# Routing of twelve of sixteen tiles moved into the attention ahead of it, in a two-layer attention and mixture-of-experts kernel

## What is computed

```
x = x + attention0(layernorm(x), ctx)      # similarity attention over 1024 context rows
x = x + experts0(layernorm(x))             # 12 gate logits a row: 8 experts, 4 "zero" experts
x = x + attention1(layernorm(x), ctx, mask)# 4 heads of 64
x = x + experts1(xf = that x)              # 8 gate logits; gelu MLP behind a layer norm per expert

logits = x_n @ gate (+ bias)               # experts0; experts1 likewise
top2, idx = top_k(logits, 2);  g = softmax(top2)
out = sum over the two picked experts of g * (act(x_n @ w1[e]) @ w2[e])
```

## Time and profile before

| | us |
|---|---|
| median of 3 runs | 1073.15 |
| lowest, highest | 1072.77, 1074.06 |
| the profiled execution | 1080.48 |
| its span, first to last instruction | 1078.5 |
| TensorE busy | 911.1 |
| VectorE busy | 624.1 |
| ScalarE busy | 511.2 |
| GpSimd busy | 421.2 |

### The profile page before, as it was taken

One profiled execution on the slowest core, in us unless ns is written; L12 is line 12 of the kernel. 1 busy time (PEld: TensorE's weight loads), 2 busy tenths in 40 slices (PEclk: granted clock), 3 DMA queues, 4 the chain that ended last, 5 costly groups with the idle time before them and its releaser, 6 DMA issues. The chain is left out here.

```text
span 1078.5 us, 19681 instructions
## 1 busy us (share of the span) xinstructions
PE 911.1 (84%) x6248; PEld 804.9 (75%) x6249; DVE 624.1 (58%) x1368; ACT 511.2 (47%) x1097; POOL 421.2 (39%) x352
## 2 busy tenths in 40 slices
PE   0579989977699997058999989897778999999996
PEld 0468979866499996047778778786648999999995
DVE  2456354326655556847878878786755444444443
ACT  1243233115344443047768767664744555555552
POOL 0445243100255553063625536321032555555542
PEclk9989999986799999579999999999689999999998
DMA  5352110007466663530001100000965666666662
GB/s 176 93 181 79 37 42 2 1 1 249 132 215 228 231 232 105 162 131 11 30 21 43 37 20 21 1 26 21 319 233 179 197 198 195 195 199 200 207 193 34
DMA packets 67570, 131.46 MB, mean 122 GB/s; under 512 B 7824, under 2 KB 50192, under 8 KB 62384
## 3 DMA queue, kind: packets, MB, share of 16 engines
q1 hardware_dynamic: 55024, 110.13, 30.0%
q0 software_dynamic: 12480, 20.48, 8.1%
HBM read 108.95 MB, written 21.64 MB: 121 GB/s over the span
## 5 line engine op out<-in xcount | busy, mean ns | idle before, releaser
L1604 PEld LDWEIGHTS d_hps<-d_xg_t,d_xw 128*128 128x128 f32 x1248 | 149.2, 196 | 7.1 <-DVE d_xg_t L1786 5.7
L1604 PE MATMUL d_hps<-d_xg_t,d_xw 128*128 128x128 f32 x1248 | 149.8, 280 | 5.0 <-DVE d_xg_t L1786 5.0
L1513 ACT ACTIVATE x<-d_hps,b 128x128 f32<-128x128 f32 x312 | 89.0, 368 | 123.9 <-PE d_hps L1604 118.9
L683 POOL TENSOR_SCALAR c_prob<-c_prob,c_rinv 128x1024 f32<-128x1024 f32 x64 | 71.4, 1123 | 140.8 <-DVE c_rinv L1083 140.4
L1614 PE MATMUL d_yps<-d_w,d_hid_hi 128*128 x312 | 116.8, 406 | 2.3 <-DVE d_hid_lo L1795 2.3
L1439 POOL DMA_INDIRECT out_x<-d_y,d_take_slot x39 | 67.3, 1725 | 111.1 <-DVE d_y L1823 60.7
L1090 DVE TENSOR_TENSOR c_pt_lo<-c_tp,c_pt_hi 128x512 fp32r<-128x512 f32 x128 | 82.1, 683 | 5.0 <-ACT c_pt_hi L939 4.7
L1617 PE MATMUL d_yps<-d_w,d_hid_lo 128*128 x312 | 82.0, 283 | 0.0
L1076 DVE CUSTOM_DVE_ANT_0 c_prob<-c_sc,c_minf 128x1024 f32<-128x1024 f32 x64 | 75.6, 1219 | 8.4 <-PE c_sc L750 6.3
L1604 PEld LDWEIGHTS b_hps<-b_xg_t,b_w 128*128 128x128 f32 x624 | 76.6, 195 | 4.6 <-issue 2.4
L1604 PE MATMUL b_hps<-b_xg_t,b_w 128*128 128x128 f32 x624 | 78.4, 280 | 1.3 <-DVE b_xg_t L1783 0.7
(11 more groups left out here) (344 smaller groups left out, 2223.7 us busy)
## 6 DMA issues: line engine op xcount, KB each, us to landing
d_xw<-in_w SPq DMA_DIRECT2D x39, 1024.0 KB
b_w<-in_w SPq DMA_DIRECT2D x47, 512.0 KB, 7.5
d_w<-in_w SPq DMA_DIRECT2D x8, 1024.0 KB, 11.6
a_raw<-in_ctx_t SPq DMA_DIRECT2D x4, 1024.0 KB, 5.4
a_raw<-in_ctx SPq DMA_DIRECT2D x4, 1024.0 KB, 5.5
ybuf<-a_zero SPq DMA_DIRECT2D x2, 2048.0 KB, 14.2
b_ysum<-ybuf SPq DMA_DIRECT2D x8, 512.0 KB, 8.3
c_ctx_t<-in_ctx_t SPq DMA_DIRECT2D x14, 256.0 KB, 3.1
```

The lines of the kernel that those rows point to most:

```text
L683: nc.gpsimd.tensor_scalar(prob[w][:], prob[w][:], rinv[:, w:w + 1], 1.0, ALU.mult, ALU.mult).then_inc(s["prob_ready"], 1)
L1513: op = nc.scalar.activation(hid[q][:, h * FH + c, :], src[:, c, :], ACT.Gelu_apprx_tanh, bias=b1[:, ds(e, 1), h * FH + c])
L1604: mm = nc.tensor.matmul(hps[j % 2][h][:, c * P:(c + 1) * P], w1[j % WL][:, k, at:at + P], xg_t[j % 2][:, k, :], start=(k == 0), stop=(k == ...
```

## The change

The sixteen tiles are split: the first TE = 12 "early" ones and four "late" ones.

1. In each attention's last steps, where the `x` of batches 0 to 2 is final, the early tiles get statistics, normalised rows (six each on VectorE and ScalarE in `attention0`; eight on ScalarE and four on VectorE in `attention1`), transposes (`turn_rows`), logits (`early_logits`) and, on VectorE, the top two (`top_two`). The rows go to DRAM from there. Square root and exponential sit in different tables of ScalarE, which are loaded for each. What routing needs (`gw`, `pick`, `top`, `idx`, `load`) now lives outside the blocks.
2. The experts blocks begin with the early tiles' ranks, while the late tiles are normalised; GpSimd makes the 24 early one-hot lanes, VectorE the eight late ones. The chain over all sixteen tiles follows as before, with `expert_of` behind the lanes.
3. `w2`'s low parts are made in order of experts: 0 to 2 on TensorE and ScalarE, 3 to 5 on VectorE, 6 and 7 on GpSimd inside the first two steps of the loop. `down` of the first six blocks waits only for its own expert's part. SyncE loads `w2` 0 and 1, the late rows, 2 to 5, then `w1` of the first blocks, then 6 and 7.
4. The scaling of `x` for the zero experts is done in steps 0 to 5 of the first loop, from `x` and its statistics (`own`, `off`).
5. To make room in `attention1` the mask is loaded tile by tile into two buffers.

```diff
+                def turn_rows(i):
+                    bank = (sc[:, 0:512], sc[:, 512:1024], tp[0][:])[i % 3]
...
+                def early_logits():
+                    pe.wait_ge(s["gate_in"], 32)
+                    for i in range(2):
+                        turn_rows(i)
+                    for i in range(TE // 2):
+                        if i + 2 < TE // 2:
+                            turn_rows(i + 2)
+                        pe.wait_ge(s["row_t"], i + 1)
+                        for a in range(2):
+                            t = 2 * i + a
+                            for k in range(KD):
+                                at = (a * KD + k) * P
+                                mm = nc.tensor.matmul(tp[1][:, t * 12:(t + 1) * 12], xn_t[i][:, at:at + P], r.gw[:, k, :],
+                                                      start=(k == 0), stop=(k == KD - 1))
+                    mm.then_inc(s["logit_done"], 1)
 
                 def step(b, q, t, before, now, nxt):
...
+                    if not now and t == 2:
+                        early_logits()
...
+                    if not now and t == 0:
+                        act.wait_ge(s["stat"], 6)
+                        nc.scalar.activation(m.std[:, slice(0, TE)], m.var[:, slice(0, TE)], ACT.Sqrt, bias=m.const[:, C_EPS:C_EPS + 1]
+                                             ).then_inc(s["sqrt_done"], 1)
+                        nc.scalar.activation(m.spare1[:], m.const[:, C_EPS:C_EPS + 1], ACT.Exp)
+                        act.wait_ge(s["stat"], 8)
+                        act.wait_ge(s["raw_lo"], 4 * B)
+                        for n in range(DVE_ROWS, TE):
+                            nc.scalar.activation(row_tile(n), m.x[:, n, :], ACT.Identity, scale=m.rstd[:, n:n + 1],
+                                                 bias=m.nmr[:, n:n + 1]).then_inc(s["row_act"], 1)
+                    if not now and t == LAST:
+                        for i in range(TE // 2):
+                            act.wait_ge(s["row_tp"], i + 1)
+                            nc.scalar.activation(xn_t[i], (sc[:, 0:512], sc[:, 512:1024], tp[0][:])[i % 3], ACT.Copy).then_inc(s["row_t"], 1)
                     if now and t == 0:
                         split_high(2 * b + 1, cn_hi[q])
...
+                def early_route():
+                    after(nc.vector.tensor_tensor(logit[:], tp[1][:, 0:TE * 12].rearrange("p (t e) -> p e t", e=12),
+                                                  r.ebias[:].unsqueeze(2).broadcast_to([P, 12, TE]), ALU.add))
+                    after(top_two(nc, m, r, after, 12, slice(0, TE), logit[:], logit2[:], grid[:]))
 
                 def step(b, q, t, before, now, nxt):
                     p, g = b - 1, b * TB + t
@@ -465,6 +574,14 @@
                             dve.wait_ge(s["pt_hi"], g * 2 + half - 1)
                             nc.vector.tensor_tensor(pt_lo[:, js, tile * P:(tile + 1) * P], tp[half][:].rearrange("p (j i) -> p j i", i=P),
                                                     pt_hi[:, js, tile * P:(tile + 1) * P], ALU.subtract).then_inc(s["pt_lo"], 1)
+                    if not now and t == 0:
+                        dve.wait_ge(s["bn_done"], B - 1)
+                        stats_chain(nc, m, dve, s["stat"], s["sqrt_done"], slice(0, TE))
+                        nc.vector.scalar_tensor_tensor(m.nmr[:, slice(0, TE)], m.mean[:, slice(0, TE)], -1.0, m.rstd[:, slice(0, TE)],
+                                                       ALU.mult, ALU.mult).then_inc(s["stat"], 1)
+                        dve.wait_ge(s["raw_lo"], 4 * B)
+                        for n in range(DVE_ROWS):
+                            normalise(nc, m, row_tile(n), n).then_inc(s["row_dve"], 1)
                     if now:
...
+                def early_logits(q):
+                    pe.wait_ge(s["row_t_act"], q + 1)
+                    pe.wait_ge(s["row_t_dve"], q + 1)
+                    for t in range(TB):
+                        n = q * TB + t
+                        for k in range(KD):
+                            mm = nc.tensor.matmul(sc[0][:, n * E:(n + 1) * E], row_t[q][:, k, t * P:(t + 1) * P], r.gw[:, k, :],
+                                                  start=(k == 0), stop=(k == KD - 1))
+                    mm.then_inc(s["logit_done"], 1)
+
                 pe.wait_ge(s["xn_ready"], TB)
                 for k in range(KD):
                     turn_x(k, tp[k])
@@ -880,17 +1035,35 @@
                     if more:
                         pe.wait_ge(s["k_lo"], b * 4 + 6)
                         q_proj(0, xb)
+                    else:
+                        pe.wait_ge(s["x_ready"], b * 2)
+                        turn_rows(0, 0, xb[:])
                     turn(b, 6, 0)
                     values(b, 4)
+                    if not more:
+                        pe.wait_ge(s["row_t_act"], 1)
+                        turn_rows(0, 1, xb[:])
                     turn(b, 6, 1)
 
                 turn(B - 1, 7, 0)
+                pe.wait_ge(s["row_t_dve"], 1)
+                pe.wait_ge(s["max_done"], B * UP * 2)
+                turn_rows(1, 0, xb[:])
                 values(B - 1, 5)
+                turn_rows(1, 1, sc[1][:, 0:512])
                 turn(B - 1, 7, 1)
+                pe.wait_ge(s["row_t_act"], 2)
+                turn_rows(2, 0, xb[:])
                 values(B - 1, 6)
+                pe.wait_ge(s["row_t_dve"], 2)
+                turn_rows(2, 1, sc[1][:, 0:512])
+                pe.wait_ge(s["gate_in"], 16)
+                early_logits(0)
+                early_logits(1)
                 values(B - 1, 7)
+                early_logits(2)
...
+                    if not more:
+                        act.wait_ge(s["stat_e"], 6)
+                        nc.scalar.activation(m.std[:, early], m.var[:, early], ACT.Sqrt, bias=m.const[:, C_EPS:C_EPS + 1]
+                                             ).then_inc(s["sqrt_e"], 1)
+                        nc.scalar.activation(m.spare1[:], m.const[:, C_EPS:C_EPS + 1], ACT.Exp)
                     head_part(b, 2)
                     if more:
                         x_high(b + 1, 1, xb)
@@ -1030,16 +1219,24 @@
                     if more:
                         k_high(b + 1, 0, 1, xb)
                     high_parts(b, 5, 1)
+                    if not more:
+                        row_norm(0)
 
                     if more:
                         q_high(b + 1, 0, xb)
...
+                    if not more:
+                        new_stats(b - 1)
+                        dve.wait_ge(s["bn_done"], B - 1)
+                        stats_to_var(nc, m, dve, s["stat_e"], early)
...
+                    if not more:
+                        var_to_rstd(nc, m, dve, s["stat_e"], s["sqrt_e"], early)
+                        nc.vector.scalar_tensor_tensor(m.nmr[:, early], m.mean[:, early], -1.0, m.rstd[:, early],
+                                                       ALU.mult, ALU.mult).then_inc(s["stat_e"], 1)
...
+                def weights_low(e):
+                    pool.wait_ge(s["w2_hi"], e + 1)
+                    pool.wait_ge(s["w2_lo"], e)
+                    nc.gpsimd.tensor_tensor(w2[:, e, :, 1, :], w2[:, e, :, 1, :].bitcast(F32), w2[:, e, :, 0, :],
+                                            ALU.subtract).then_inc(s["w2_lo"], 1)
+
+                pool.wait_ge(s["lane_e_ready"], 1)
+                for k in range(2):
+                    for t in range(TE):
+                        apart(m, pool)
+                        op = nc.gpsimd.tensor_scalar(in_lane[:, k * T + t, :], c16(C_ROW, P), lane[:, k, t:t + 1], 1.0,
+                                                     ALU.is_equal, ALU.mult)
+                op.then_inc(s["in_lane_e"], 1)
+                pool.wait_ge(r.rows_out, r.rows_total)
+                pool.wait_ge(s["xn_out"], 16)
                 pool.wait_ge(s["slot_ready"], 1)
                 for n in range(GATHERS):
                     gather(n)
+                for e in POOL_LOW:
+                    weights_low(e)
                 if not first:
...
                     result(n, j, turn)
+                    if first and last and n < STEPS:
+                        for t in range(n * T // STEPS, (n + 1) * T // STEPS):
+                            V.tensor_scalar(m.x[:, t, :], m.x[:, t, :], own[:, t:t + 1], off[:, t:t + 1],
+                                            ALU.mult, ALU.add).then_inc(s["x_ready"], 1)
```

456 lines of the change are left out of this document (286 added, 170 removed).

## The result

The changed kernel is slower: 1091.24 us as the median of 4 runs (1090.89 to 1094.05), the kernel before beside it 1073.61 (1072.77 to 1078.14). The ratio is 1.0161, 95% interval 1.0128 to 1.0195. The profiled execution took 1094.05 us for a span of 1092.2, that of before 1080.48 for 1078.5, so the traces show 13.7 of the 17.6 us.

The account below looks back on a forecast made before the run. Routing around the expert loops, chains of small VectorE instructions of some 45 and 62 us, was taken as the price to cut. First layer -8.9 and second 0.0 sum to -8.9 us: 1064 from a median of 1073.15, range 1052 to 1077.

Parts of the forecast that it names:

- rival C: Both experts blocks: late first w1 weights, or small GpSimd lanes at 0.7 us, shrink the gain by 8: 1072; chance 0.12.
- A: Stretch from start to first experts block: early logits ahead of the first attention's last projection cost +5.6 us.
- Rival D: Second attention's end: TensorE's waits drop the clock to 1.2 GHz, 14 us of matmuls become 28: 1078; chance 0.13.
- The first loop: First experts loop: moved scaling costs +2.4 us, GpSimd's low parts holding VectorE +1.6 (0 to 4).
- `up(0)` behind `take_slot`: First experts block: first `up` follows `take_slot` by 5.4 us as before, if its weights have landed.
- The second attention: Second attention's units 5 and 7 and drain: early routing work costs +14.9 us, bounds 8 and 22.
- The gate wait: Second experts block, before `down(1)`: gates queued behind GpSimd's low parts hold VectorE, then TensorE: +6.3 us (0 to 9).
- rival E: Second layer: GpSimd's low parts hold up VectorE in both loops' starts, and with the gates lose 6: 1070; chance 0.07.
- E: Stretch from the second block's `down(0)` to the end: costs +6.3 us.
- B: Stretch from the first experts block's start to its `up(0)`: 26.5 us, not 45.0, a gain of 18.5.
- C: Stretch from the first block's `up(0)` to the second experts block (loop, sums, second attention): costs +18.9 us.
- D: Stretch from the second experts block's start to its `down(0)`: 41.0 us, not 62.2, a gain of 21.2.

Follow-up runs that it names:

- e1_lanes: Changed kernel with only the 12 first-pick early lanes on GpSimd, the second picks' made by VectorE: 1085.55 us, ratio 1.0104.
- e4_wide: Changed kernel with early logits of both attention ends multiplying repeated gate columns (60 and 64 wide, not 12 and 8): 1083.07 us, ratio 1.0080.
- e3_scale: Changed kernel with the sixteen instructions that scale x back at the first loop's end: 1085.42 us, ratio 1.0088.
- e5_four: Changed kernel with four edits: 12 early lanes on VectorE, gates ahead of w2's low parts, scaling at loop's end, wide logits: 1072.98 us, ratio 0.9984.
- e6_five: As e5_four, with w2's low parts of experts 6 and 7 made by VectorE instead of GpSimd in both layers: 1065.95 us, ratio 0.9912.
- e12_w1late: As e6_five, but in the first experts block the second and third w1, and w2 behind them, wait for the first gather: 1066.76 us, ratio 0.9879.
- e9_w2late: As e6_five, but w2's experts 6 and 7 and the second layer's b2 load only after the first gather landed: 1065.22 us, ratio 0.9898.
- e2_gates: Changed kernel with GpSimd taking the second block's first three gates ahead of w2's low parts of experts 6 and 7: 1090.8 us, ratio 1.0132.

## Why the prediction was wrong

**The side.** I gave 1064 and a range up to 1077; it was 1091. The shape of the argument holds (routing gets shorter, the attentions' ends longer, a gate wait appears), and each piece was priced too well: -8.9 against +13.7 us in the spans. That is 22.6 of the 27 us between forecast and median. Two of the three signs that I had named for being wrong came: GpSimd's lanes end the wait of the slots, and the clock falls in the attention's drain. The third, the first `up` waiting for w1, did not. The steps that failed, and at the end one that held:

1. "The 24 early lanes on GpSimd are costed at nothing." A lane takes 0.71 us and, beside VectorE's products, up to 2.04. I had named the point from which it decides, 0.7, and a price of 4 us (rival C); it was 4.6 in the first block (e1_lanes). That 4 comes so near is partly luck: the slots could start at 20.1 us and not at 17.9, which makes the lanes cheaper, and two of them lost 2.6 us beside VectorE, which I had left out. The step behind it was wrong: I argued from a rate per element (7.2 us for all), but 1024 elements in 1.12 us (the page's mean for the normalising of `c_prob`, a like instruction in another type) and 128 in 0.71 mean that nearly all of a small one, some 0.65 us by the slope between the two, an estimate, doesn't depend on its size.
2. The clock. "The clock is at half level behind that wait in any case" priced A, and for D of the rivals "slice 27, the drain as it was, shows a 9" spoke against a fall. In A I had counted the low clock as already paid for, and in the drain not at all. It fell in both ends while TensorE was busy, on the logits themselves. Wide logits give back 3.3 and 3.1 to 5.4 us (e4_wide and the kernels built on it). Rival D had the right place and consequence, the wrong cause (waits of TensorE, which are there in e4_wide too), and with 14 us too high a price.
3. The first loop: +2.4 for the scaling and +1.6 for GpSimd's low parts. Measured +4.9 (e3_scale) and +3.0 (e5_four to e6_five), less what the two share, +5.9 in all. The mechanism was right, the size off: I left out what the clock costs: behind TensorE's wait of 2.17 us the next `up` took 3.58 us, and behind the 1.65 of e3_scale 1.95. The row that I priced GpSimd's hold by was also misread: the 5.54 us of `normalise` lie beside two instructions of GpSimd, 2.40 us at 95.74 and 2.45 at 98.07, and not beside one.
4. `up(0)` behind `take_slot`: 5.4 us predicted in the first block, 7.7 measured (284.27 less 276.57). From its issue to the transpose of what it brought the first gather took 3.0 us before (281.93 to 284.91) and 5.3 after (277.77 to 283.06). Now the loads of w1 lie over it, as e12_w1late shows against e9_w2late; in the second block 9.1 where I took 6.4 (31.7 less 25.3). No row of before shows a gather with such loads over it, and I took the old price over. Rival C had w1 itself landing 5 us late; it didn't, but it made the gather late.
5. The second attention: +14.9, measured +19.2. Without the clock's 3.1 to 5.4 it is 13.8 to 16.1, so the sum over units 5 and 7 and the drain was good. Its table loads on ScalarE:

```profile
728.30 1.28 ACT L1204 ACT_TABLE_LOAD   x1
729.60 0.30 ACT L1204 ACTIVATE std<-var,const 128x12 f32<-128x12 f32 x1
729.92 1.28 ACT L1206 ACT_TABLE_LOAD   x1
731.22 0.20 ACT L1206 ACTIVATE spare<-const 128x1 f32<-128x1 f32 x1
```

Each load costs 1.30 us until the next instruction starts, and no idle time lies before or behind it (the instruction ahead, at 728.10, takes 0.19); I had taken 1.28, and not the 2.66 us with a drain that the Trainium skill gives (ScalarE: Activation LUTs, What ACT_TABLE_LOAD costs); by that the sum would have been worse in this term.

6. The gate wait: +6.3 predicted, 6.70 measured, and 1.7 more for a `down` at the lower clock. Right, as everything ahead of it came some 5 us late alike. But behind it stood a second one, VectorE held by GpSimd, which the sum didn't need and any repair did (e2_gates). It is rival E's mechanism; with the gates mended it costs 3.0 us in the first loop and 5.6 in E (e5_four to e6_five).

**The remainder, by stretch.** A missed by 2.1 us, with the clock's 3.3 in it. At the upper level it is 4.0 on TensorE (19.2 us from `bexp` to the last projection in e4_wide, 15.3 before), near my lower bound of 3.7. B missed by 8.8: lanes 4.6, gather 2.3, the rest in small steps (`load` 1.1 late, `expert_of` 1.5). C missed by 5.5: the loop 1.9, the second attention 4.3, the sums -0.8. D missed by 5.2: `up(0)` 3.7 late, of which the gather 2.7 and GpSimd's lanes 1.0, and 10.8 us from there to `down(0)` where I took 9.3, because `up(0)` still ran at the lower clock (5.82 in place of the 4 that I took). E missed by 1.1: wait and clock together are 2.1 over, and 1.0 the other way has no row here.

Three sums of the prediction are off in themselves. `take_slot` at 21.3 and 5.4 behind it are 26.7, not 26.5. The four terms of the second block (9.2, 4.1, 3.4, 1.3) are 18.0, not 18.7, which changes nothing, as TensorE's low parts decide there. And with clock and gap as they were D would be 62.2 less 31.7 and 15.9, -14.6, not -15.6; that the measured -16.0 lies near the latter is chance, as `up(0)` was later and the gap was gone.

The Trainium skill's rule that I quoted (GPSIMD Engine Reference, Key points, on the interfaces that GpSimd shares with VectorE) holds, and more strictly than I priced it: VectorE's subtraction with two SBUF operands isn't merely somewhat slower, it ends 0.6 us behind GpSimd's instruction, about what it takes alone (5.02 us for 0.68, e2_gates). Two scalings with one tensor from SBUF each, 2.75 in place of some 0.7, fared alike. The rule as quoted names two inputs or a certain mode; these have one input from SBUF, and whether they run in that mode no run here shows.

## What to carry to other kernels

Work that is moved to an idle engine has a price per instruction there, to be read from a small instruction of that engine, not from the rate of a large one; and where the two engines hold each other up, as here (5.02 us for 0.68 on VectorE, 2.04 for 0.71 on GpSimd), the price comes back on the engine that was to be relieved. A stretch of narrow matmuls on a busy TensorE can cost clock for itself and for what stands right behind it, and making them wider cost next to nothing here. Where a wait is found, look what else is queued behind it before pricing its repair: of the 8 us of one wait only 2.7 came back until the second cause was gone.

## What the runs showed of the hardware that was not expected

- TensorE's granted clock fell to its lower level, 1.2 GHz, while the engine was busy without a gap, in both attention ends, with logits of 12 and 8 columns (0.50 from 230 to 236 and from 759 to 772), and stayed at 2.4 GHz with 60 and 64 columns in the same places (1.00 from 221 to 240 and from 751 to 762, e4_wide).
- A comparison of 128 elements in bf16 took GpSimd 0.71 us in the median, and up to 2.04; VectorE needed 0.18 for the same.
- VectorE and GpSimd held each other up in both directions; what was held ended 0.6 to 0.7 us behind the other engine's instruction, about its own time: 5.02 us for 0.68 on VectorE (e2_gates), 2.04 for 0.71 on GpSimd (the changed kernel, from 264.9, VectorE's product being over at 266.2).
- A gather's landing time followed what the queues carried: 3.4 us from its issue to the transpose with one w1 of 0.5 MB over it (270.31 to 273.74, e12_w1late), 6.6 with three (269.98 to 276.60, e9_w2late).
